# A fused attention and expert layer on one core: routing products placed singly between the attention's steps, and sums divided apart from their copy

## The reference

```python
qkv = (x @ qkv_w + qkv_b).reshape(b, s, HEADS, 3 * HEAD_DIM).transpose(0, 2, 1, 3)
q, k, v = jnp.split(qkv, 3, axis=-1)
q, k = rot(q), rot(k)
attn = jax.nn.softmax(jnp.einsum('bhqd,bhkd->bhqk', q, k) / HEAD_DIM ** 0.5, axis=-1)
out = jnp.einsum('bhqk,bhkd->bhqd', attn, v).transpose(0, 2, 1, 3).reshape(b, s, -1)
x = layernorm(x + out @ out_w + out_b)

n = layer_norm(x, g1, be1)
x2 = x + n + (n @ mix_w + mix_b)
flat = layer_norm(x2, g2, be2)
probs = jax.nn.softmax(flat @ router_w, axis=-1)
topw, topi = jax.lax.top_k(probs, 2)
h = jax.nn.silu(jnp.einsum('td,edf->tef', flat, w1) + b1)
y = jnp.einsum('tef,efd->ted', h, w2) + b2
x = layernorm(x + x2 + jnp.einsum('te,ted->td', combine, y))   # combine: topw at the two chosen experts
```

## Time and profile before

| | us |
|---|---|
| median of 3 runs (1684.42 to 1687.19) | 1686.78 |
| the profiled execution's own time | 1684.99 |
| its span | 1683.3 |
| TensorE matmuls busy in the span | 1615.5 (96%) |
| ScalarE busy | 1246.2 (74%) |
| VectorE busy | 535.5 (32%) |
| GpSimd busy | 469.8 (28%) |

### The profile page before, as it was taken

One profiled execution on the slowest core, in us unless ns is written; L12 is line 12 of the kernel. 1 busy time (PEld: TensorE's weight loads), 2 busy tenths in 40 slices (PEclk: granted clock), 3 DMA queues, 4 the chain that ended last, 5 costly groups with the idle time before them and its releaser, 6 DMA issues.

```text
span 1683.3 us, 45804 instructions
## 1 busy us (share of the span) xinstructions
PE 1615.5 (96%) x17940; PEld 929.7 (55%) x17941; DVE 535.5 (32%) x1442; ACT 1246.2 (74%) x1871; POOL 469.8 (28%) x495
## 2 busy tenths in 40 slices
PE   7999999999999989999999999999999999999990
PEld 5543333433433435433433433458999999999990
DVE  4551125425525525435425535525310000000004
ACT  5649999999999989999999999963444444444441
POOL 4630001202202202112202202115455444444441
PEclk9989999999999999999999999999999999999996
DMA  4775210101101354601101100646568666566645
GB/s 164 206 157 89 60 39 15 50 24 34 49 27 31 71 78 71 135 26 34 49 24 34 49 27 30 240 132 178 161 190 223 181 187 191 182 184 186 176 117 206
DMA packets 108487, 181.18 MB, mean 108 GB/s; under 512 B 14121, under 2 KB 80361, under 8 KB 108137
## 3 DMA queue, kind: packets, MB, share of 16 engines
q1 hardware_dynamic: 95010, 160.88, 33.1%
q0 software_dynamic: 13296, 17.77, 5.7%
HBM read 134.07 MB, written 40.18 MB: 104 GB/s over the span
## 4 chain that ended last, share of the span: by engine, by line
PE 81%; issue 5%; ACT 5%; DMA 1%; DVE 1%; POOL 0%; POOLq 0%; ACTq 0%; DVEq 0%
PE at_s L1376 24%; PE at_po L1388 23%; PE at_s L1499 14%; PE at_s L1512 14%; ACT place L1288 4%; PE at_small L1404 4%; DMA rows_out<-place,at_v 1%; PE at_small L1397 1%; PE at_po L1488 1%; DVE cb_ln_stats L696 1%; DVE place L1728 0%; DMA place<-rows_out 0%; POOL place L1242 0%; POOL place L1247 0%; POOLq L1240 0%
## 5 line engine op out<-in xcount | busy, mean ns | idle before, releaser
L1288 ACT ACTIVATE place<-at_s 128x1024 f32<-128x1024 f32 x1024 | 956.1, 1142 | 42.2 <-PE at_s L1376 41.7
L1376 PE MATMUL at_s<-place 99*32 99x512 bf16 x8192 | 582.3, 382 | 13.9 <-ACT place L1288 6.6
L1388 PE MATMUL at_po<-place,at_v 128*32 128x512 f32 x4096 | 536.3, 594 | 0.9 <-ACT place L1288 0.9
L1376 PEld LDWEIGHTS at_s<-place 99*32 99x32 bf16 x8192 | 202.0, 95 | 481.5 <-issue 222.6
L1499 PEld LDWEIGHTS at_s<-place 128*128 128x128 f32 x2272 | 265.8, 193 | 4.2 <-issue 0.8
L1305 ACT ACTIVATE place<-at_s,b_turned 128x128 f32<-128x128 f32 x568 | 162.5, 369 | 141.1 <-PE at_s L1499 138.5
L1499 PE MATMUL at_s<-place 128*128 128x128 f32 x2272 | 266.8, 276 | 0.0
L1512 PE MATMUL at_s<-place 128*128 x1136 | 256.9, 379 | 0.5 <-ACT place L1305 0.5
L1512 PEld LDWEIGHTS at_s<-place 128*128 128x128 f32 x1136 | 210.4, 190 | 26.5 <-issue 0.7
L1388 PEld LDWEIGHTS at_po<-place,at_v 128*32 128x32 f32 x4096 | 128.8, 111 | 105.1 <-ACT place L1288 2.2
L1321 ACT ACTIVATE place<-at_s,at_v 128x256 f32<-128x256 f32 x71 | 33.7, 474 | 162.0 <-PE at_s L1512 159.7
(11 more groups left out here) (213 smaller groups left out, 957.3 us busy)
## 6 DMA issues: line engine op xcount, KB each, us to landing
place<-in_w SPq DMA_DIRECT2D x79, 1024.0 KB, 10.1
place<-k_parts SPq DMA_DIRECT2D x48, 256.0 KB, 6.0
place<-q_parts SPq DMA_DIRECT2D x192, 64.0 KB
at_v<-rows_in SPq DMA_DIRECT2D x71, 129.0 KB
place<-in_x SPq DMA_DIRECT2D x8, 512.0 KB, 4.5
at_heads_T<-at_o SPq DMA_DIRECT2D x128, 32.0 KB
rt_x_in<-in_x SPq DMA_DIRECT2D x8, 512.0 KB, 4.1
rows_out<-rt_total SPq DMA_DIRECT2D x8, 512.0 KB, 5.9
```

Source lines behind the costliest of these rows:

```text
L1288: nc.scalar.activation(probs[:, slot(n), :], p_s[n % BUFFERS][:, :], ACT.Exp).then_inc(exp_done, 1)
L1376: last = nc.tensor.matmul(p_s[n % BUFFERS][j:j + 32, s * 512:(s + 1) * 512], k_rows[0:ROWS_M, quad(q).start + h, kt * P + j:kt * P + j + 3 ...
L1388: last = nc.tensor.matmul(p_o[32 * h:32 * h + 32, :], v_one[q % 2][:, h, kt, :], probs[:, slot(q * NG + g), s * 512:(s + 1) * 512], start= ...
```

## The change

Three things move. Each product of four pieces is issued one piece at a time, in every second step, in place of two pieces at a time; so a half takes four steps' places rather than two, and the steps of all later parts of the routing but the count change with it (four transposes stay one unit). VectorE's `copy_out` is split in the copy and `divide`. And VectorE's order in `route` changes: for quarter 0 the copy stands before x1's layer norm and the division after the turned copies; for quarter 1 both stand between the two halves of x2, after the first. The wait for `repacked` is done at the first piece of the first half alone. `TAIL_AT` names the new steps at the same tiles.

```diff
-    OUT_AT = {14: (0, 0), 16: (0, 2), 18: (1, 0), 20: (1, 2)}
-    NORM_AT = {48: 0, 52: 1}
-    MIX_AT = {56: (0, 0), 58: (0, 2), 60: (1, 0), 62: (1, 2)}
-    SENT_AT = {80: 0, 84: 1}
-    ROUTER_AT = {88: 0, 90: 4}
+    OUT_AT = {14: (0, 0), 16: (0, 1), 18: (0, 2), 20: (0, 3), 24: (1, 0), 26: (1, 1), 28: (1, 2), 30: (1, 3)}
+    NORM_AT = {53: 0, 55: 1}
+    MIX_AT = {58: (0, 0), 60: (0, 1), 62: (0, 2), 64: (0, 3), 68: (1, 0), 70: (1, 1), 72: (1, 2), 74: (1, 3)}
+    SENT_AT = {88: 0, 90: 1}
+    ROUTER_AT = {93: 0, 95: 4}
...
                         half, first = OUT_AT[at]
-                        if first == 0:
+                        if half == first == 0:
                             for u in range(2):
                                 pe.wait_ge(repacked[u], (i + 1) * UNITS * (8 * QUAD))
-                        return product(out_w, heads_T, (2 * half, 2 * half + 1), D, job, (first, first + 1))
+                        return product(out_w, heads_T, (2 * half, 2 * half + 1), D, job, (first,))
...
                     v.tensor_copy(o_sb[q % 2][:, :], p_o[:, :]).then_inc(o_copied, 1)
+
+                def divide(i, q):
+
+                    unit = i * UNITS + q
                     dve.wait_ge(o_copied, unit + 2)
...
                     add_total(x1, 0)
                     add_total(x1, 1)
+                    if beside:
+                        copy_out(i + 1, 0)
                     dve.wait_ge(small_read, job.first + job.n + 1)
                     layer_norm(v, steps, x1, x1, w)
-                    if beside:
-                        copy_out(i + 1, 0)
                     layer_norm(v, steps, norm1, x1, w)
...
                     turned_half(0)
                     turned_half(1)
+                    if beside:
+                        divide(i + 1, 0)
                     dve.wait_ge(total_ready, i * 2 + 2)
                     add_total(x2, 0)
+                    if beside:
+                        copy_out(i + 1, 1)
+                        divide(i + 1, 1)
                     add_total(x2, 1)
                     dve.wait_ge(small_read, job.first + job.n + 1)
                     dve.sem_inc(x2_ready, 1)
-                    if beside:
-                        copy_out(i + 1, 1)
-                    else:
+                    if not beside:
                         v.tensor_tensor(total[:, :, :], x1[:, :, :], x2[:, :, :], ALU.add).then_inc(kept, 1)
...
                     if beside:
                         copy_out(i + 1, 2)
+                        divide(i + 1, 2)
```

More of the change, by code:

```diff
@@ L927, in attend_route_experts @@
         TAIL_TURNS = 3
-        TAIL_AT = {2: (14, 16), 3: (18, 20), 9: (48,), 10: (52,), 11: (56, 58), 12: (60, 62),
-                   17: (80,), 18: (84,), 19: (88, 90), 26: (118,)}
+        TAIL_AT = {2: (14, 16, 18, 20), 3: (24, 26, 28, 30), 9: (53,), 10: (55,), 11: (58, 60, 62, 64),
+                   12: (68, 70, 72, 74), 17: (88,), 18: (90,), 19: (93, 95), 26: (118,)}
         SEND_ROUNDS = {0: (3, 5, 8, 10, 13, 15), 1: (18, 21)}
@@ L1442, in route @@
                         half, first = MIX_AT[at]
-                        return product(mix_w, turned, (2 * half, 2 * half + 1), D, job, (first, first + 1))
+                        return product(mix_w, turned, (2 * half, 2 * half + 1), D, job, (first,))
                     elif at in SENT_AT:
@@ L1700, in _ @@
                     copy_out(0, q)
+                    divide(0, q)
                 dve.wait_ge(loaded_w, 16 * 9)
@@ L1705, in _ @@
                     copy_out(i - 1, UNITS - 1)
+                    divide(i - 1, UNITS - 1)
                     route(i - 1, steps, job, True)
@@ L1710, in _ @@
                 copy_out(LAST - 1, UNITS - 1)
+                divide(LAST - 1, UNITS - 1)
                 making = Chain(dve, made)
@@ L1716, in _ @@
                 copy_out(LAST, UNITS - 1)
+                divide(LAST, UNITS - 1)
                 route(LAST, steps, job, False)
```

## The result

| | before | after |
|---|---|---|
| median of 20 runs each, us | 1685.59 (1682.28 to 1689.94) | 1687.88 (1683.95 to 1692.94) |
| ratio after to before | | 1.0018, 95% interval 1.0010 to 1.0026 |
| the profiled execution, us | 1684.99 | 1684.97 |
| its span, us | 1683.3 | 1683.3 |

What follows compares the result with a forecast made beforehand. TensorE was taken to set the pace while products run, ScalarE otherwise. Per group -0.4 -0.3 -0.1 -0.2 +0.8 = -0.2 us, -0.22 before rounding, times seven -1.5 us: median 1685.3 us, range 1678 to 1689.5.

Steps and rivals of the forecast that it cites:

- same: Whole run within 0.2%, that is within 3.4 us of 1686.8; chance 0.67.
- Output product: Steps 14 to 31: spreading single pieces cuts the loss from 2.7 to 2.3 us, gain 0.4 per group.
- Mix product: Its loss of 3.1 us falls to 2.74 when spread; gain 0.3 taken per group.
- the wait at step 66: TensorE stands 0.8 us per group for VectorE's copy of quarter 1, now behind an addition; bounds 0 and 1.6.
- Rival (a): The wait at step 66 is hidden: -1.02 us per group, -7.1 in all, 1679.7 us; chance 0.19.
- Rival (b): VectorE's addition starts 0.7 us late, wait at step 66 is 1.5: +4.8 us, 1691.6; chance 0.08.
- Step 98: Next quarter's start, its copy behind two short logit instructions: covered by TensorE's lead, cost 0 to 0.2 us, taken as 0.
- First transposes: Steps 53 and 55, before 48 and 52: loss 0.8 us against 0.85, gain 0.1 per group.
- Second transposes and router: Steps 88, 90, 93, 95: loss 0.9 us against 1.1, gain 0.2 per group; the L1636 wait goes.
- stall that is gone at step 80 of group 4: TensorE's 1.5 us stall with DMA engines full could go or come back elsewhere: plus or minus 1.5 us once.
- Rival (c): The clock falls to half at each new wait: seven times, +12 us, so 1695; chance 0.02.
- the rule of the Trainium skill: Brief idling between matmul groups can swing the clock, so the new wait would cost a slow stretch in each group.

Runs made afterwards that it cites:

- the longer wait: The changed kernel with one more copy of the whole accumulator (0.69 us) ahead of the copy of quarter 1: group 125.44 us, 0.63 more.
- sets apart: Kernel with copies of quarters 1 and 2 moved ahead (123.63 us a group), transposes at 52, 55, 86, 90, router at 94, 98: group 123.45 us.

## Why the prediction was wrong

The range (1678 to 1689.5) holds the median, and "same" came out by the 0.2% bound, but neither bears the sum out. The forecast was wrong in its sign per group: -0.22 foretold, +0.66 measured. The steps that failed are the cost at step 98, taken as 0 and measured at 0.39, and the gains at the two places of transposes, 0.08 and 0.23, which are a loss of 0.10 and one of 0.17. By its steps:

1. **Output product, right.** -0.39 foretold, -0.40 measured; the loss to step 33 was to be 2.3 and to step 36 is 2.34. The exponentials come in pairs with 1.24 us between them, as said.
2. **Mix product and the wait at step 66, right, in their sum.** Forecast -0.3 and +0.8, together +0.48; measured +0.52. Apart, the product gains 0.39 (3.06 to 2.67) and the wait costs 0.91. The gap at step 69 was to be 1.6 to 1.7 and is 1.68. Rival (a) is refuted by the longer wait: it is on the path one to one. Rival (b)'s late addition did not come: the addition starts 0.32 us behind the product (427.73 to 428.05), against 0.25 in the earlier trace rows. Its size, 0.7 a group slower with 0.2 at step 98, came nearest, but by another mechanism, so that this is luck.
3. **Step 98, wrong.** The step of the sum was "the lead there covers it (a cost of 0 to 0.2; I take 0)". It is 0.39, twice the bound. I counted the two logit instructions, but not when the router's second piece ends. It moved from step 90 to step 95, which is the quarter's last round, and the next quarter's first round is three steps on. The copy behind the logits therefore could start only 1.28 us behind that product's start, with 0.69 to run. And the lead, which was to cover it, covered only about 0.16; that the pieces at 88, 90, 93 and 95 had spent the rest is my reading and wasn't tested. This is the same pattern as at step 66, which I had priced with care. I had not gone through the second place by the same starts and ends.
4. **First transposes, wrong.** -0.08 foretold, +0.10 measured. I worked out 0.8 for after, from durations, and set it against 0.85 read from the trace of before. A sum on one side and a reading on the other: the whole error of the sum goes into the difference. The set is 0.69, not 0.59, so the same formula gives 2 x 0.69 - 0.4 = 0.98 for after (0.95 measured), and for before, with one more pair of steps between the sets, 0.9 (0.85). The pair of steps lost between them is the +0.10; "sets apart" got it back.
5. **Second transposes and router, wrong,** by the same slip. 0.9 worked out for after stood against 1.1 read. With sets of 0.69 and the router's two pieces at 0.27 (459.25 to the scores at 459.52) in place of 0.23, after is 2 x 0.69 + 2 x 0.27 - 0.4 - 0.3 = 1.22, and 1.16 is measured once the copy is out of the way. It is 0.16 to 0.17 more than before, not 0.2 less. The 0.4 us waits for L1636 that went away seem to have cost little: before, with them, this stretch lost 0.99 in all. How much of them TensorE's lead had covered wasn't measured by itself.
6. **The rest.** The stretch 104 to 128 gained 0.10; forecast nothing, and the cause is open.

The steps that were wrong add up: 0.39 (step 98), 0.18 (first transposes) and 0.39 or 0.40 (second ones and router) are 0.97; with +0.04 from the mix product and -0.10 at the end, and 0.01 less from the output, the difference from -0.22 to +0.68 is explained to 0.02 us.

**From a group to the run.** Seven times 0.66 is 4.6 us, and the runs show 3.0, with 4.4 at the interval's end. The stall that is gone at step 80 of group 4 would take 1.8 of it: 2.8, an estimate, since the kernel before was profiled only once. The prediction had this stall as plus or minus 1.5 us, in no sum. What is left can't be attributed, for the stalls of groups 3 and 4 vary by more from one execution to the next (253.4 and 256.8 for one kernel). No half clock came in groups 1, 2, 5 or 6. Rival (c) thus did not come (its 1695 counts from the profiled 1683.5; from the median's 1685.3 it would be 1697), and the rule of the Trainium skill weighed beside it, that short idle times between groups of matmuls can make the clock swing ("TensorE: Matmul & The Clock Gate", section "A second HAM failure mode: psum-queue depth-cycling"), did not show here: two stalls of up to 0.72 us a group left the clock at 1.00, and so did one of 1.31 in the kernel with the longer wait. The last group took its 124.8 us, without a stall on DMA.

**What the spreading is worth,** then: without the two waits it is 0.52 us a group faster than before (123.63), and in every third step 0.86 (123.29). The waits it brought, 0.91 and 0.39 together 1.3 (1.18 by whole groups), are more than twice that first gain.

## What to carry to other kernels

When work is spread over more steps, every accumulator that is handed over in the new stretch must be looked at anew, and each by its own starts and ends: here two copies, held by 0.69 and by 0.73 us of small work ahead of them, turned a gain of 0.5 us per group into a loss of 0.66, and moving them ahead gave nearly all of it back (1.18 us of 1.3). Work out both sides of a difference by the same formula, never one side from durations and the other from the trace. And where run times scatter by some us while a steady loop repeats within 0.05, measure the loop.

## What the runs showed of the hardware

- A lone set of four 128x128 fp32 transposes between other matmuls takes 0.69 us of TensorE's queue, a second set right behind it 0.43: a quarter of a microsecond goes in the change to and from them. In the kernel before a lone set took the same (0.54 in place of 0.43 from the scores ahead to the set, then 0.59).
- A wait of TensorE shown as 0.72 us cost 0.91 in its stretch. The profile counts it from the modelled end of the last matmul: the row of two steps' scores shows 1.03 us, and from start to start they take 0.86. A second one, shown as 0.35, held the queue for some 0.55 and cost 0.39.
- Two 128x512 copies in a row on VectorE start 0.60 us apart, though each shows 0.68 to 0.69.
- Where the weights of a round follow a wait for two engines, the profile named GpSimd (0.81 us), which had ended 0.77 us earlier; with VectorE's copy moved, that wait was gone.
- At group 4's first product the spacing of the exponentials is 2.9 us in one execution of the changed kernel and 5.3 in the next. The kernels with the sets or the mix product later had none in group 3 (123.2 to 123.6 us), nor had the one with the copy of quarter 1 first; whether that is the tables' doing or luck was not tried.
- TensorE's stall at that product and the clock: after 3.1 us (before) the granted clock was 0.50 for 3.4 us, after 2.3 us (the changed kernel, first execution) it stayed at 1.00.
